# Placing the second half of the tokens between the expert units' steps

## The reference

```python
logits = norm(x) @ router               # [8192 tokens, 8 experts]
best two experts of each token, gates = softmax over the two logits
y = sum over the two of gate * expert(norm(x))
# gelu layer: expert(u) = gelu(u @ W1[e] + b1[e]) @ W2[e] + b2[e], width 512
# silu layer: expert(u) = (silu(u @ w1[e].T) * (u @ w3[e].T)) @ w2[e].T, width 341
x = x + y
```

## Time and profile before

| what | us |
|---|---|
| median of 3 runs (1573.67 to 1580.92) | 1574.26 |
| the profiled execution | 1575.33 |
| span of its instructions | 1573.5 |
| PE busy | 1217.1 (77%) |
| DVE busy | 964.4 (61%) |
| ACT busy | 545.5 (35%) |
| POOL busy | 572.9 (36%) |

### The profile page before, as it was taken

How to read it: one execution, slowest core, us unless ns; L and a number is a source line. 1 busy time by engine, 2 the same in 40 slices (tenths; PEclk the granted TensorE clock), 3 DMA queues, 4 the chain that set the end, 5 groups by cost and what they waited for, 6 DMA issues and landing times. The chain is left out here.

```text
span 1573.5 us, 31944 instructions
## 1 busy us (share of the span) xinstructions
PE 1217.1 (77%) x11770; PEld 1058.2 (67%) x11770; DVE 964.4 (61%) x2351; ACT 545.5 (35%) x1247; POOL 572.9 (36%) x643
## 2 busy tenths in 40 slices
PE   6999988468581999879896584757549999999940
PEld 3555547468580999879894354535539999998940
DVE  3777763798654444435543775686556777887731
ACT  3444431064350555434453341432313233222220
POOL 4000000100235666655502552045516640556654
PEclk9999997779555999989997796679559999999975
DMA  7700000000401333233324220011103332333341
GB/s 270 281 0 1 1 1 3 4 1 0 128 21 59 100 119 115 85 105 106 105 70 104 51 67 17 1 32 41 42 27 97 112 103 72 110 103 103 88 140 53
DMA packets 87887, 115.45 MB, mean 73 GB/s; under 512 B 18693, under 2 KB 70272, under 8 KB 87744
## 3 DMA queue, kind: packets, MB, share of 16 engines
q1 hardware_dynamic: 66784, 62.73, 13.0%
q0 software_dynamic: 20960, 50.76, 10.2%
HBM read 53.01 MB, written 60.42 MB: 72 GB/s over the span
## 5 line engine op out<-in xcount | busy, mean ns | idle before, releaser
L1302 POOL DMA_INDIRECT sorted_rows<-s_normed,s_places x128 | 138.1, 1079 | 164.5 <-DMA sorted_rows<-s_normed,s_places 51.8
L1378 POOL DMA_INDIRECT sx_fetch<-sorted_results,s_places x128 | 135.6, 1059 | 142.3 <-DMA sx_fetch<-sorted_results,s_places 62.8
L1302 POOL DMA_INDIRECT sorted_rows<-g_normed,g_places x128 | 134.3, 1049 | 106.9 <-DMA sorted_rows<-g_normed,g_places 48.8
L1461 PE MATMUL g_bank<-weights,gx_hT 128*128 x1360 | 168.7, 278 | 0.6 <-issue 0.6
L1461 PEld LDWEIGHTS g_bank<-weights,gx_hT 128*128 128x128 f32 x1360 | 161.5, 195 | 1.2 <-issue 1.2
L1378 POOL DMA_INDIRECT gx_fetch<-sorted_results,g_places x128 | 124.7, 974 | 102.4 <-DMA gx_fetch<-sorted_results,g_places 71.0
L1426 PE MATMUL s_bank<-sx_xT_high,sx_w_now 128*128 128x256 f32 (+1 forms) x510 | 151.6, 297 | 1.8 <-DVE sx_hT L1531 1.2
L1428 PE MATMUL s_bank<-sx_xT_high,sx_w_now 128*128 128x256 f32 (+1 forms) x510 | 143.9, 282 | 0.0
L1427 PE MATMUL s_bank<-sx_xT_low,sx_w_now 128*128 128x256 f32 (+1 forms) x510 | 143.8, 282 | 0.0
L1486 ACT ACTIVATE gx_hT<-g_bank,gx_b_now 128x256 f32<-128x256 f32 x340 | 133.1, 482 | 3.0 <-PE g_bank L1461 3.0
L1461 PE MATMUL s_bank<-weights,sx_hT 128*128 (+1 forms) x1020 | 130.5, 278 | 3.5 <-issue 1.7
(11 more groups left out here) (409 smaller groups left out, 2792.0 us busy)
## 6 DMA issues: line engine op xcount, KB each, us to landing
sorted_rows<-zeros POOLq DMA_DIRECT2D x29, 512.0 KB, 16.6
gx_xq<-sorted_rows SPq DMA_DIRECT2D x85, 128.0 KB, 2.1
sorted_results<-gx_yq SPq DMA_DIRECT2D x85, 128.0 KB, 1.9
sx_xq<-sorted_rows SPq DMA_DIRECT2D x85, 128.0 KB, 2.1
sorted_results<-sx_yq SPq DMA_DIRECT2D x85, 128.0 KB, 2.0
feats<-in_x SPq DMA_DIRECT2D x8, 512.0 KB, 6.2
out<-s_normed SPq DMA_DIRECT2D x16, 256.0 KB, 3.8
g_raw_up<-in_L_ffn_W SPq DMA_DIRECT2D x1, 2048.0 KB, 9.1
```

Of the source, the lines that this page charges most:

```text
L1302: pool.indirect_dma_start(out=sorted_rows[g], out_offset=bass.IndirectOffsetOnAxis(ap=places[:, at, r:r + 1], axis=0), in_=normed[:, at, : ...
L1378: pool.indirect_dma_start(out=fetch[n % 2][:, i, r, :], out_offset=None, in_=self.sorted_results[g], in_offset=bass.IndirectOffsetOnAxis(a ...
L1461: done = pe.matmul(down[u % 2][:, P * k:P * k + C], hT[u % 2][0:width, i, P * k:P * k + P], self.w_down[0:width, bass.ds(e, 1), i, :].rear ...
```

## The change

- `Route.place` becomes a generator, `place_in_pieces`, that stops after each two or so operations. For part 1 VectorE runs one piece at the end of each unit step, from step 0 on, in both expert layers. In step `COUNT` = 7 TensorE does the two counting products, ScalarE takes the exponentials, and VectorE copies both results out of the PSUM banks that the units use. The routing blocks end after the last scores (gelu: after the adjusting of the logits, `adjust`).
- In both layers the sends of part 1's groups wait for `placed` to reach 2, that is for the piece at the end of step 12. For gelu this is group 2 alone; for silu it is groups 1 and 2. TensorE waits for part 1's owners before its first `go_down` in them.
- Gelu's group 0 is sent with no waits between the DMAs (`pauses=False`). All other sends and fetches keep theirs.
- The tiles of `Route` outlive the routing block; for gelu they share a room with two tiles of the window attention. `PartNorm` takes its parts as a list. Neither adds an instruction.

```diff
+    def take_totals(self, dve, part):
+        dve.wait_ge(self.counted, 2 * part + 2)
+        self.steps.then(dve.tensor_copy(self.count[:, :], self.totals[part][:, 0:E * PT]))
+    def take_ahead(self, dve, part):
+        self.steps.then(dve.tensor_copy(self.held[part][:, :], self.ahead[part][:, 0:E * PT]))
+    def place_in_pieces(self, dve, steps, part):
...
         for r in range(2):
 
             steps.then(dve.tensor_reduce(best[r][:, :], logits[:, :, :] if r == 0 else work[:, :, :],
                                          AX.X, ALU.max))
             steps.then(dve.tensor_tensor(masks[r][:, :, :], logits[:, :, :] if r == 0 else work[:, :, :],
                                          best[r][:, :].unsqueeze(2).to_broadcast(over_e), ALU.is_ge))
+            yield
             steps.then(dve.tensor_tensor(masks[r][:, :, :], masks[r][:, :, :], ranks, ALU.mult))
             steps.then(dve.tensor_reduce(first[:, :], masks[r][:, :, :], AX.X, ALU.max))
+            yield
             steps.then(dve.tensor_tensor(masks[r][:, :, :], masks[r][:, :, :],
                                          first[:, :].unsqueeze(2).to_broadcast(over_e), ALU.is_equal))
             if r == 0:
                 steps.then(dve.scalar_tensor_tensor(out=work[:, :, :], in0=masks[0][:, :, :], scalar=-BIG,
                                                     in1=logits[:, :, :], op0=ALU.mult, op1=ALU.add))
+                yield
...
         dve.tensor_tensor(best[1][:, :], best[1][:, :], best[0][:, :], ALU.subtract).then_inc(self.exp_asked, 1)
-        dve.wait_ge(self.counted, 2 * part + 2)
-        steps.then(dve.tensor_copy(count[:, :], self.totals[part][:, 0:E * PT]))
+        yield
+        if part in self.held:
+            yield
+        else:
+            self.take_totals(dve, part)
...
+            dve.tensor_copy(self.owners[:, at], self.owner_f[:, at]).then_inc(self.owned, 1)
+            dve.wait_ge(self.owned, g + 1)
+            yield
...
-        if at % 2 == 1:
+        if at % 2 == 1 and pauses:
             pool.wait_ge(sent[g], (at + 1 - plan.first_tile[g]) * 2 * 16)
...
         def go_down(u):
+            if route and u == self.plan.first_unit[self.plan.parts[1][0]]:
+                pe.wait_ge(route.owned, self.plan.groups)
...
             if s < self.NU:
                 done = turn(s)
+            if route and s == self.COUNT:
+                pe.wait_ge(y_ready, s - self.TO_DOWN)
+                route.count_part(pe, 1)
...
             if 0 <= s - self.TO_UP < self.NU:
                 act_hidden(s - self.TO_UP)
+            if route and s == self.COUNT:
+                route.exponents(act, 1)
...
+        placing = route.place_in_pieces(dve, route.steps, 1) if route else iter(())
         for s in range(self.STEPS):
             dve.wait_ge(self.stepped, s + 1)
+            if route and s == self.COUNT:
+                route.take_totals(dve, 1)
             if s >= self.TO_DOWN:
                 take_down(s - self.TO_DOWN, experts.pop(s - self.TO_DOWN))
+            if route and s == self.COUNT:
+                dve.wait_ge(self.x_high, s + 1)
+                route.take_ahead(dve, 1)
...
             for n in adds.get(s, ()):
                 self.add_result(dve, n)
+            next(placing, None)
...
```

In gelu's routing block and in its units' block:

```diff
-                send_group(pool, plan, 0, normed, places, group_rows, sent)
+                send_group(pool, plan, 0, normed, places, group_rows, sent, pauses=False)
-                route.count_part(pe, 1)
-                route.exponents(act, 1)
-                route.place(dve, steps, 1)
+                route.adjust(dve, steps, 1)
...
-            for g in range(1, plan.groups):
-                send_group(pool, plan, g, normed, places, group_rows, sent)
+            send_group(pool, plan, 1, normed, places, group_rows, sent)
+            pool.wait_ge(route.placed, 2)
+            send_group(pool, plan, 2, normed, places, group_rows, sent)
```

More of the change, by code:

```diff
@@ L1033, in finish, with __init__ @@
                                  ).then_inc(self.ready, 1)
-        dve.wait_ge(self.ready, part + 1)
+        dve.wait_ge(self.ready, piece + 1)
 class Route:
-    def __init__(self, t, kind, plan, by_vector, router, rbias, ident, tokens, normed, gates, places, owners, tag):
+    def __init__(self, t, kind, plan, by_vector, router, rbias, ident, tokens, normed, gates, places, owners, tag, pieces, brief, held=()):
         self.kind, self.plan, self.router, self.rbias, self.ident = kind, plan, router, rbias, ident
@@ L1050, in __init__ @@
         self.share = by_vector
-        self.norm = PartNorm(t, tag, twice=kind.gelu)
-        self.uT = [t.sbuf(f"{tag}uT{i}", [P, N]) for i in range(2)]
         self.logits = t.sbuf(f"{tag}logits", [P, PT, E])
@@ L1074, in __init__ @@
         self.part_i = [t.sbuf(f"{tag}part{i}", [P, PT, 2], I32) for i in range(2)]
+        self.held = {part: t.sbuf(f"{tag}ahead{part}", [P, E * PT]) for part in held}
+        self.norm = PartNorm(brief, tag, kind.gelu, pieces)
+        self.uT = [brief.sbuf(f"{tag}uT{i}", [P, N]) for i in range(2)]
         self.constants = t.sem(f"{tag}constants")
@@ L1194, in place @@
         dve.wait_ge(self.score_taken, (part + 1) * PB)
-        if kind.gelu:
-            steps.then(dve.tensor_tensor(logits[:, :, :], logits[:, :, :],
-                                         norm.root[1][:, all_tiles].unsqueeze(2).to_broadcast(over_e), ALU.mult))
-            steps.then(dve.tensor_tensor(logits[:, :, :], logits[:, :, :],
-                                         self.rbias[:, :].unsqueeze(1).to_broadcast(over_e), ALU.add))
+        if kind.gelu and part not in self.held:
+            self.adjust(dve, steps, part)
+            yield
         for r in range(2):
@@ L1246, in place @@
         steps.did(dve.tensor_tensor(flat(shift), flat(shift), flat(total), ALU.subtract))
-        steps.then(dve.tensor_tensor(before[:, :], before[:, :], self.ahead[part][:, 0:E * PT], ALU.add))
+        steps.then(dve.tensor_tensor(before[:, :], before[:, :], self.held.get(part, self.ahead[part])[:, 0:E * PT], ALU.add))
+        yield
         for i, g in enumerate(groups):
@@ L1779, with __init__ @@
 class WindowAttention:
-    def __init__(self, t, tag, tables, tokens, first, end, banks, spare):
+    def __init__(self, t, tag, tables, tokens, first, end, banks, spare, share=None):
         self.tables, self.tokens, self.first, self.end = tables, tokens, first, end
@@ L2261, in _ @@
         def _(act):
-            units.scalar(act)
+            units.scalar(act, route=route)
             window.scalar(act, setup=silu_setup)
```

138 lines of the change are left out of this document (92 added, 46 removed).

## The result

The changed kernel took 1558.45 us (median of 4 runs, 1555.65 to 1561.73) against 1575.41 us for the kernel before, run beside it (4 runs, 1573.67 to 1580.92): ratio 0.9887, 95% interval 0.9855 to 0.9919. Run again beside 23 runs of the kernel before, it took 1554.97 us against 1574.31: ratio 0.9897, interval 0.9868 to 0.9926. So it is 16 to 19 us faster (by the ratios 17.8 and 16.2, by the medians 17.0 and 19.3), where 18.7 were forecast; the forecast time was 1555.6. The profiled execution took 1558.14 us, its span 1556.3.

A forecast was written before the change was run, and what follows sets the result against it. POOL was taken to bound the kernel, its end moving one to one with the start of silu's fetches; 9.6 + 18.9 - 11.7 + 1.85 = 18.7 us off 1574.26 gives 1555.6 us, range 1549 to 1566.

The forecast's parts named there:

- Gelu's start, 9.6: Gelu's routing block: group 0 without pauses saves 8.7 us between sends and 0.9 before the drain, 9.6 in all.
- Rival A: Gelu's group 0: the unpaused sends wait in their queue, so the 9.6 us are lost; 1565.2 us, chance 0.10.
- Gelu's pieces, 0: Gelu's unit steps: placing in pieces costs nothing, `placed` coming 8.3 us before POOL is ready for group 2.
- Silu's routing end, 18.9: Silu's routing block: ends at VectorE's copy of the scores instead of the gates, so the first load comes 18.9 us earlier.
- Silu's lateness: Silu's unit steps: pieces make VectorE 4.9 us late at step 12, so `placed` is 2 at 55.9 us after the first load.
- B: Silu's unit steps: the pieces cost nothing and POOL gains 4.9 us more; 1550.7 us, chance 0.13.
- C: Silu's unit steps: VectorE is later than forecast; double lateness gives 1560.5 us, up to 1566 with late rows; chance 0.10.
- D: Silu's steps 6 to 12: holds cost TensorE its clock, `placed` comes at 76, time 1576 us or more; chance 0.03.
- The sends, 117.1: Silu: POOL's sends of groups 1 and 2 take 117.1 us and end 173.1 us after the first load, fetches following.
- The stores at 166.7: Silu: the units' stores are in by 166.7 us after the first load at the latest, before POOL's sends end.
- The 1.85 us that come back: Silu's fetches: the seventeenth's 3.69 us wait for VectorE shrinks to an ordinary pause, returning about 1.85 us.
- The sum: Whole kernel: 9.6 + 18.9 - 11.7 + 1.85 = 18.7 us off, forecasting 1555.6 us.

The follow-up runs named there:

- the silu experiments: Changed kernel with silu's second half placed in its routing block (0.9938), its pieces two a step (0.9886), or its pieces three steps later (0.9943).
- before again: The kernel before, run again unchanged for a second profile; 1582.3 us in that one execution.
- group 0 unpaused: Kernel before with only gelu's group 0 sent without pauses; 1568.8 us, ratio 0.9964.
- silu in its block: Changed kernel with silu's second half placed in the routing block again; 1562.5 us, ratio 0.9938 to the kernel before.
- changed again: The changed kernel run again unchanged, with a second profile; 1554.97 us, ratio 0.9897 to the kernel before.
- gelu in its block: Changed kernel with gelu's second half placed in the routing block again; 1554.4 us, ratio 0.9886 to the kernel before.
- adds later: Changed kernel with VectorE's gelu adds begun six steps later (52 and 66 for 46 and 60); 1541.5 us, ratio 0.9815 to the kernel before.

## Why the prediction was right

- **What bounds.** Right: the silu experiments show the end following the fetches' start, and the chain after names the sends.
- **Gelu's start, 9.6.** Measured 10.3 in the profile. Idle time between the sends: from 18.05 us to 9.45, so 8.6 (forecast 8.7). The last wait: from the last send's end to the first send of group 1, 5.0 us before and 3.6 after, so 1.4 and not 0.9. The sends' own time: 0.25 us less, which was put at nothing. Its reason was a misreading of the earlier trace rows: "0.96 each" is 12.42 us over 13 sends, but the window cuts the last of them off, and one of the 13 (481.50) took 1.34 us. Rival A falls: the sends stand 0.30 apart to the last. The drain was forecast to begin 0.5 us after the last send; it is issued 14 us ahead of it.
- **Gelu's pieces, 0.** Right: group 2's first send waited for a landing (1.81 us), not for `placed`. `places` was complete 47.6 us after the first load (VectorE's last operation on it ends at 539.12), the prediction has 47.5; 6.7 us to spare, forecast 8.3.
- **Silu's routing end, 18.9.** The first pair of profiles shows 18.8 (138.36 to 119.60). Over four profiles of each kind (placing in the block: before, before again, group 0 unpaused, silu in its block; in pieces: changed, changed again, gelu in its block, adds later) the means are 139.6 and 118.8, so 20.7.
- **Silu's lateness.** This term was too large. The sum had 4.9 + 0.3 = 5.2 us of it by step 12, of which 4.2 would show in TensorE's steps and 1 only in VectorE. TensorE was 3.8 us late at the end of step 12, and from there to the end of piece 12 it took 4.4 us, as the sum has it (3.2 + 1.2): VectorE was not late beyond that. So the first send of group 1 came at 54.8, forecast 56.0. Rivals B and C fall: B had no lateness, C twice as much. D too: from 1160 to 1200 the granted clock was 1.00.
- **The sends, 117.1.** Measured 117.7 (1197.45 to 1315.17). Fetches from 172.6, forecast 173.1. The stores at 166.7 "at the latest": 165.4 to 166.1 where POOL waited for them with one piece a step, 169.7 with two.
- **The 1.85 us that come back.** Not found. The seventeenth fetch waits 1.92 instead of 3.69, but POOL's waits for landings and adds within silu's fetches sum to 67.4 us, against 66.8 before: other waits grew (the one before the twenty-fifth fetch from 1.84 to 2.80). Over the four profiles of each kind the fetches take 0.9 us more, not 1.85 less.
- **The sum.** It came out partly by luck. Over the same profiles silu nets 20.7 - 10.8 - 0.9 = 9.0 against 9.05 forecast, but of three terms that are each off by 0.9 to 2.8 us. With gelu's 10.3 that makes 19.3, and 16.2 to 19.3 were timed. The first pair of profiles comes to its 17.2 by another way: silu 6.7, gelu's start 10.3, gelu's later columns 3.7 lost, and 4.2 that lie ahead of anything changed.

"Whatever POOL gains is passed on whole" was right for this change, but its reason was read too narrowly: 8.78 us of TensorE's wait looked like all that could be won. It was 27.

## What to carry to other kernels

When an engine issues transfers and waits for each handful, count its pauses before anything else: here the waits after every fourth (1.54 us for sends, 2.2 in the mean for fetches, 0.30 where nothing is waited for) were worth 76 us with all that hung on them (1555.0 to 1478.9). The wait that the profile names first isn't the price of being late: the same lateness comes back behind an engine that stands in order before an add, and only pushing that add away, or the transfer forward, shows how much. And where work is moved out of a serial block, price what it then holds up: the sends, not VectorE's own time, took back half of silu's gain.

## What the runs showed of the hardware that was not expected

- 32 indirect sends in a row take 1.28 us each in the mean from start to start (39.66 us for 31), 1.26 for the last ones: no slowing. Fetches without waits take 1.25 to 1.26 in the median. A landing wait in the fetches is 2.1 to 2.2 us in the mean whether four or eight were issued before it.
- The drain after group 0 is issued 14 us before the last send starts (473.5 against 487.67) once nothing pauses them, and ends 2.7 us after its end; before, it lasted 2.67 us from its issue.
- POOL's unpaused sends beside VectorE's placing took 1.2 us more for 32 (40.9 against 39.7), in both kernels that had them together. Which of the placing's operations cost it wasn't tried. The Trainium skill, "SBUF — State Buffer" (Who interferes with whom), holds that copies, casts and tensor-scalar operations in a two-port mode block POOL's descriptor writing. The trace does not put the cost there: sends beside the CAST and TENSOR_SCALAR before `places` took 0.96 us, and the lengthened ones, 1.06 to 1.30 us, stand mostly beside tensor-tensor and reduce operations (472.7 to 481.1 with group 0 unpaused only). In the kernel before, three sends beside such operations took 0.95 to 0.96 and the next 1.34, so the kind of operation alone doesn't explain it; the cause is open.
- TensorE's granted clock was 1.00 when it stopped for rows at 650.7 and 0.50 when it went on at 659.3; it stayed at 0.50 until 665.9, while TensorE worked, from 661 on without a break, and was 1.00 after that.
